# Four-layer graph network: base products in pairs and a ring of five single banks for the combining product

## The reference

```python
weight = jnp.einsum('rb,bio->rio', w_comp, bases)   # 32 relations out of 8 bases
xw = jnp.einsum('ni,rio->nro', h, weight)           # 6250 x 32 x 256
msg = xw[src, rel_type] * norm
out = jax.ops.segment_sum(msg, dst, num_segments=h.shape[0])
return jax.nn.relu(out)
```

## Time and profile before

| what | us |
|---|---|
| median of 3 runs | 6327.82 (6323.94 to 6328.81) |
| the profiled execution, its own time | 6325.51 |
| its span in the profile | 6323.4 |
| `layer0`: first combine starts, last copy to the table | 99.3 and 760.2 |

### The profile page before, as it was taken

One profiled execution on the slowest core, in us unless ns is written; L12 is line 12 of the kernel. 1 busy time (PEld: TensorE's weight loads), 2 busy tenths in 40 slices (PEclk: granted clock), 3 DMA queues, 4 the chain that ended last, 5 costly groups with the idle time before them and its releaser, 6 DMA issues.

```text
span 6323.4 us, 84221 instructions
## 1 busy us (share of the span) xinstructions
PE 4999.2 (79%) x22753; PEld 3570.0 (56%) x22754; DVE 3927.4 (62%) x9519; ACT 1545.8 (24%) x3075; POOL 3595.8 (57%) x3549
## 2 busy tenths in 40 slices
PE   5999789999987777776666666279999996677676
PEld 4888767777763334333444444158878774333333
DVE  5555566666656666666666666866666665556555
ACT  2555434444440000001222222123333331000000
POOL 0000067777757777776777777233333335777776
PEclk8999989999997777777888888689999997666666
DMA  4777756666654444445777777167777764444443
GB/s 159 317 323 317 306 187 216 216 217 218 217 187 122 125 123 124 124 123 170 241 243 244 245 242 246 60 209 244 236 235 237 242 232 133 115 117 116 117 116 111
DMA packets 406354, 1228.70 MB, mean 194 GB/s; under 512 B 130482, under 2 KB 205212, under 8 KB 355029
## 3 DMA queue, kind: packets, MB, share of 16 engines
q1 hardware_dynamic: 245509, 781.00, 34.5%
q0 software_dynamic: 160464, 443.17, 24.6%
HBM read 636.81 MB, written 587.04 MB: 194 GB/s over the span
## 4 chain that ended last, share of the span: by engine, by line
PE 65%; DVE 11%; issue 9%; POOL 6%; DMA 5%; SPq 2%; DVEq 1%; ACT 1%; POOLq 0%; ACTq 0%
PE ps L1420 27%; PE ps L1595 11%; PE ps L1444 8%; PE ps L1578 5%; PE ps L1381 5%; PE ps L1398 4%; POOL A L638 3%; POOL ring L638 3%; DMA work<-place_dram 2%; DVE W L823 2%; DVE A L823 2%; SPq L484 1%; DMA A<-gat_table,ix 1%; PE ps L1493 1%; DVEq L789 1%
## 5 line engine op out<-in xcount | busy, mean ns | idle before, releaser
L626 POOL DMA_INDIRECT ring<-table,idx x2490 | 2364.4, 950 | 1603.8 <-DVEq L847 741.8
L1420 PE MATMUL ps<-ring,W 128*128 128x256 f32 x3320 | 1202.7, 482 | 425.4 <-DVE W L823 265.9
L1420 PEld LDWEIGHTS ps<-ring,W 128*128 128x128 f32 x3320 | 693.7, 232 | 856.8 <-issue 399.4
L823 DVE TENSOR_SCALAR W<-iota,dloc,norm 128x128 f32<-128x128 f32 x1660 | 599.7, 362 | 766.3 <-PE ps L1420 757.2
L1420 PE MATMUL ps<-ring,A 128*128 128x256 f32 x1660 | 713.3, 538 | 275.4 <-DVE A L823 214.4
L651 POOL TENSOR_TENSOR ring<-ring,work 128x1024 f32<-128x1024 f32 x208 | 405.7, 1951 | 807.4 <-DMA ring<-rows_dram 807.3
L1595 PE MATMUL ps<-W_r,work_r 128*128 128x512 f32 x1960 | 701.6, 441 | 0.0
L841 DVE TENSOR_TENSOR X<-X,ps 128x256 f32 x1660 | 687.3, 414 | 13.7 <-PE ps L1420 10.8
L1420 PEld LDWEIGHTS ps<-ring,A 128*128 128x128 f32 x1660 | 338.8, 247 | 615.7 <-DVE A L823 368.3
L1444 PE MATMUL ps<-W_r,work_r 128*128 128x512 f32 x1568 | 560.9, 440 | 0.0
L1155 DVE TENSOR_TENSOR X<-X,ps 128x264 f32 x830 | 352.4, 425 | 330.8 <-PE ps L1578 275.0
(11 more groups left out here) (231 smaller groups left out, 7316.3 us busy)
## 6 DMA issues: line engine op xcount, KB each, us to landing
ring<-rows_dram SPq DMA_DIRECT2D x208, 528.0 KB, 4.7
table<-A SPq DMA_DIRECT2D x50, 2048.0 KB, 9.6
table<-A SPq DMA_DIRECT2D x98, 1024.0 KB, 4.5
table<-X SPq DMA_DIRECT2D x48, 2048.0 KB, 10.1
table<-A SPq DMA_DIRECT2D x49, 1280.0 KB, 5.5
table<-W SPq DMA_DIRECT2D x49, 1280.0 KB, 7.0
rows_dram<-ring SPq DMA_DIRECT2D x52, 1056.0 KB, 4.7
rows_dram<-A SPq DMA_DIRECT2D x52, 1056.0 KB, 4.6
```

What stands on the lines that cost most here:

```text
L626: pool.indirect_dma_start(out=f_ring[:, s % NR, :], out_offset=None, in_=src, in_offset=bass.IndirectOffsetOnAxis(ap=idx[:, s:s + 1], axis ...
L823: return dve.tensor_scalar(marks_[:, k % G, :], iota[:, :], dloc[:, k:k + 1], norm[:, k:k + 1], ALU.is_equal, ALU.mult).then_inc(wk.onehot ...
L1420: pe.matmul(ps[:, s % banks, 0:D], marks_[:, s % G, :], f_ring[:, s % NR, :], start=True, stop=True).then_inc(wk.step_done, 1)
```

## The change

It has two parts. `L_BASES` now gives base products in pairs: q = 0 and 1 after turn 8 of k, q = 2 and 3 after turn 12, 4 and 5 after turn 16, 6 and 7 after turn 20. The three engines walk the pair one after the other at that place, so four combines follow each other between pairs. And the combine's banks are taken one by one out of a ring of five, banks 3 to 7 (bank 7 was not used in this phase). Bank 3 + (2t + s) % 5 of turn t's s = 0 was last used by turn t - 3's s = 1, which VectorE empties, and that of s = 1 by turn t - 2's s = 0, which ScalarE empties. So the wait for ScalarE stays at turn t - 2 and the wait for VectorE goes back to turn t - 3. No instruction is added or removed.

```diff
--- before.py
+++ after.py
@@ -258,7 +258,7 @@
 
         L_TURNS = [(k, w, q) for k in range(NSB) for w in range(blocks_of(k)) for q in range(OQ)]
         L_AT = {turn: t for t, turn in enumerate(L_TURNS)}
-        L_BASES = {L_AT[k, 0, 0] + (6, 8, 10, 12, 14, 16, 18, 20)[q]: (k + 1, q) for k in range(NSB - 1) for q in range(OQ)}
+        L_BASES = {L_AT[k, 0, 0] + 8 + 2 * q: ((k + 1, q), (k + 1, q + 1)) for k in range(NSB - 1) for q in range(0, OQ, 2)}
 
         def freed_by(m):
 
@@ -323,7 +323,7 @@
             return l_table[w][:, :, q * 4 * OS + s * 2 * OS:q * 4 * OS + (s + 1) * 2 * OS].rearrange("p r (h o) -> p h r o", h=2)
 
         def comb_bank(t, s):
-            return ps[:, 3 + 2 * (t % 2) + s, :]
+            return ps[:, 3 + (2 * t + s) % 5, :]
 
         block = ctx.enter_context(nc.Block())
 
@@ -780,8 +780,8 @@
                     low_xb(0, q)
                 for t, (k, w, q) in enumerate(L_TURNS):
                     to_table(t)
-                    if t in L_BASES:
-                        low_xb(*L_BASES[t])
+                    for k_, q_ in L_BASES.get(t, ()):
+                        low_xb(k_, q_)
                     if w == 0 and q == 4 and k + 1 < NSB:
                         low_x(k + 1)
 
@@ -1209,8 +1209,8 @@
                     high_xb(0, q)
                 for t, (k, w, q) in enumerate(L_TURNS):
                     to_table(t)
-                    if t in L_BASES:
-                        high_xb(*L_BASES[t])
+                    for k_, q_ in L_BASES.get(t, ()):
+                        high_xb(k_, q_)
                     if w == 0 and q == 4 and k + 1 < NSB:
                         high_x(k + 1)
 
@@ -1389,7 +1389,8 @@
                         pe.wait_ge(xb_low, OQ * k + q + 1)
                     if t >= 2:
                         pe.wait_ge(l_act, t - 1)
-                        pe.wait_ge(l_dve, t - 1)
+                    if t >= 3:
+                        pe.wait_ge(l_dve, t - 2)
                     terms = [(l_high, comb_high), (l_low, comb_high), (l_high, comb_low)]
                     for h in range(2):
                         for n, (rows, c) in enumerate(terms):
@@ -1407,8 +1408,8 @@
                     base_products(0, q)
                 for t, (k, w, q) in enumerate(L_TURNS):
                     combine(t)
-                    if t in L_BASES:
-                        base_products(*L_BASES[t])
+                    for k_, q_ in L_BASES.get(t, ()):
+                        base_products(k_, q_)
                     if w == 0 and q == 3 and k + 1 < NSB:
                         turn_x(k + 1)
```

## The result

| | us |
|---|---|
| changed kernel, median of 12 runs | 6310.17 (6307.29 to 6317.11) |
| kernel before, median of 12 runs | 6325.70 |
| ratio | 0.9977, 95% interval 0.9968 to 0.9986 |
| predicted | 6317.0, range 6305 to 6329 |

The change gains 15.5 us, 0.23%, where 10.8 were forecast. It is just over the 0.2% that I had taken as the limit. The time lies in the stated range but outside the 6312 to 6323 of rival A, the forecast itself: it is the time of rival B. One run of the kernel before took 7116 us; it counts as slow and is left out of the ratio.

A forecast was written before the change was run, and what follows sets the result against it. TensorE, busy 98 of 100 us in the first layer, bounds the stage. Savings of 37.4 and 12.7 less new waits of 23.0 and 16.3 give 10.8 us less: median 6317.0, range 6305 to 6329.

The forecast's parts named there:

- rival A: First layer: the forecast itself, third combine of each four waits about 0.3 us; range 6312 to 6323, chance 0.62.
- rival B: Third combines wait less for ScalarE's copy: released 0.07 us sooner gives 6309, no wait 6278; chance 0.22.
- C3: Third of four successive combines; forecast to wait for ScalarE's copy of the first, 0.31 to 0.32 us in most groups.
- fewer changes of kind: TensorE between combines and base products: 96 pairs instead of 192 sets, 0.39 us each, 37.4 us less.
- the late low half: Base products of q = 0 no longer wait for the transposed nodes' low half: 24 x 0.53, 12.7 us less.
- C3 in three groups of each k: Third combines wait for the bank ScalarE empties of the first: 72 x 0.32, 23.0 us more.
- the group behind the split: Turns 5 to 8, after the transposed nodes' split: third combine loses 0.43, fourth 0.25; 24 x 0.68, 16.3 us more.
- first and last k beyond one k's share: Ends of the layer: shorter waits at the last three combines and the longer run at the first about cancel.
- its time of 6344: TensorE drain of 128 cycles, 0.053 us, two per pair: only 10.2 us saved, time near 6344.
- C: The gap between combines and base products stays per set or shrinks only partly: 6354, slower; chance 0.08.
- D: Table stores take over: landings 1 us beyond what the pair hides hold up ScalarE, then TensorE; 24 us, 6341; chance 0.04.
- E: The ring does not free the third combine, VectorE's copy still decides: 44 us, hence 6361; chance 0.04.

The follow-up runs named there:

- earlier split alone: Kernel before, with ScalarE and VectorE splitting the transposed nodes after turn 3 instead of turn 4: 6315.08 us, ratio 0.9980.
- four banks: Changed kernel with the ring undone, base products still in pairs but combines on the four banks of before: 6372.36 us, ratio 1.0070.
- both its versions with five banks and one moved step: Changed kernel with the transposition moved behind the pair after turn 4, ratio 0.9956; changed kernel with transposed nodes split after turn 3, ratio 0.9968.
- six banks: Changed kernel with the transposition beside the pair and in bank 1, combines on six banks: 7156.75 us beside 7195.73, ratio 0.9950.

## Why the prediction was right, and what of it was not

The signs and mechanisms of all four forecast terms came out, and the time lies in the range. The number of rival A, the forecast itself with a wait of 0.32 for each C3, did not come: the range held because it took in B.

| step, each of layer0 as a whole | forecast | measured |
|---|---|---|
| fewer changes of kind | -37.4 | see below, consistent with 0.39 for a pair |
| the late low half | -12.7 | -11.8 (earlier split alone) |
| C3 in three groups of each k | +23.0 | +18 (72 x 0.25) |
| the group behind the split | +16.3 | +16 (24 x 0.67) |
| changes of kind behind a combine that waited | none | +3 (24 x 0.12) |
| first and last k beyond one k's share | 0 | -1.0 |
| sum | -10.8 | -14.0 |

The measured column is made of parts from several traces and closes only to about 1 us. Within one trace it closes: averaged over 22 k, one k takes 26.68 us instead of 27.22, 0.54 less, where 0.45 was forecast. Its parts are 4 x 0.39 + 0.52 - 3 x 0.25 - 0.67 = 0.66, and the 0.12 between 0.66 and 0.54 is about what the gaps of 0.23 to 0.25 add, which the prediction had at nothing. Of the 3.2 us by which the layer gained more than forecast, 2.2 lie in the 23 whole k, and 1.0 in the first and the last, which the prediction took to cancel.

*Fewer changes of kind.* A cycle of the changed kernel is 6.34. Two cycles of before are 6.48; less 0.39, with C3's measured 0.25, that is 6.34. So 0.39 holds for a pair, and the seam of two sets is even. That the gap belongs to the change between 64 and 128 rows is shown by the transposition, which has a gap beside combines and none beside base products, in two kernels. Beside combines it stands in the kernel before:

```profile
237.19 0.28 PE L1398 MATMUL ps<-ring_r,A_r 64*128 64x256 f32 x2
237.40 0.66 PE L1369 MATMUL ps<-ident,X 128*128 128x128 f32 x4
237.99 0.39 PE L1398 MATMUL ps<-ring_r,A_r 64*128 64x256 f32 x2
```

It starts 0.21 behind the last pair, and the combine 0.20 behind its last matmul (237.40 + 0.66 - 0.27 = 237.79). That this gap is the engine emptying itself is not shown by any run. Key Properties of TensorEngine Tiling (Array Packing) in the Trainium skill says that a change of the tiling mode drains TensorE, and the place of every gap agrees with it. My estimate of 0.053 from the 128 cycles of Step-by-step: what each phase is for, in TensorE: Matmul & The Clock Gate of the Trainium skill, is far below the 0.20 measured, and its time of 6344 did not come.

*The late low half.* Right in place and size. I had counted it as a by-product of the pairs, and it alone is worth most of their net gain.

*C3's wait.* Right in mechanism, and the largest mis-sized term: 0.32 forecast, 0.25 measured. I took the release behind VectorE's copy, 0.12, for ScalarE's; it is 0.05 in the second block and, in the first, 0.07 (265.79 + 0.60 = 266.39 to a first pair at 266.49 with its load 0.03 ahead). With 0.25 instead of 0.32 the sum is 15.8, and with 11.8 for the low half it is 14.9, 0.9 from the measured 14.0. This is rival B, which the prediction priced at 6309 with a chance of 0.22; 6310.17 was measured. That the time came so near B's is in part luck: the 24 fourth combines that B also counted gained nothing, since they wait for VectorE's copy, and the longer gaps, the ends and some 1.5 us outside the layer make up the number.

*The group behind the split.* Right: 0.32 + 0.07 for C3 and 0.99 - 0.78 + 0.07 = 0.28 for C4, 0.67 together; 0.68 were forecast.

*The other rivals.* C fell with the 24 loads in one row and the missing gap at the transposition. D fell: even at 338 GB/s no group of TensorE waits for a store. But one landing was waited for by 1.1 us there, so the margin is small. E is true of four banks, which lose 43.2 us against the kernel before and 57.2 against the ring, and false of the ring.

## What to carry to other kernels

Read the steps between matmuls at the seams before counting what a reordering gives: TensorE was "98% busy" and still lost 0.2 us at each change between work on 64 and on 128 rows. Moving one transposition beside work of its kind gave as much as the whole change or more (17.6 and 14.0 us), though over half of it was a wait that the move also took away. When an edit moves several things, undo each alone: here the removal of one wait that the pairing did not aim at is worth 11.8 us by itself, beside 14.0 for the whole. And a longer run of one kind needs more banks: four made it lose 43 us, five gain 14.

## What was not expected of the hardware

A TensorE load that waits on a copy's semaphore came 0.05 to 0.07 us after the end of ScalarE's copy (the changed kernel and both its versions with five banks and one moved step) and 0.12 after VectorE's (the kernel before, four banks, six banks). Why the two differ is not shown. A wait that ends just in time for the first pair to start in step still costs 0.08 to 0.10 at the second pair (six banks: 0.20 instead of 0.118). In the rows the waited load starts together with its pair, where inside a combine loads start 0.11 ahead; that this is the cause is my reading. Where the last combine before a change of kind had waited, the change cost 0.02 to 0.04 more. And the profile puts such waits down to "issue" or to an engine long done, so they are found by the steps and not by the list of waits.
